# Expert stage of a ViT layer: 31 blocks of 256 rows and nine units of 128 rows in place of 39 blocks, four blocks beside the last pair's chain

## The reference, cut to what matters

```python
h = tok(x, W, gamma)                                  # 16 x 256 tokens, E = 256
h = h + attn(layernorm(h), Wq, Wk, Wv, Wg, Wa, ba, Wo, gn_w, gn_b)
xf = layernorm(h).reshape(4096, 256)
probs = softmax(xf @ w_router)                        # 8 experts
topk_w, topk_idx = top_k(probs, 2)
weights = sum(topk_w[..., None] * one_hot(topk_idx, 8), axis=1)
hid = gelu(einsum('te,ieh->tih', xf, w1) + b1)        # 256 -> 1024
y   = einsum('tih,ihe->tie', hid, w2) + b2            # 1024 -> 256
h = h + sum(y * weights[..., None], axis=1)
```

## Time and profile before

| | |
|---|---|
| median of three runs | 1410.64 us (1409.53 to 1412.68) |
| the profiled execution, its own time | 1410.71 us |
| its span in the profile | 1408.9 us |
| mean granted clock of TensorE | 0.975 of full speed |
| TensorE matmuls | 1296.7 us busy, 92% of the span, 9012 instructions |
| DVE | 923.7 us, 66% |
| ACT | 935.0 us, 66% |
| POOL | 458.5 us, 33% |
| HBM | 166.01 MB read, 29.96 MB written |
| weights of the experts | 78 loads of 1024 KB, median 7.3 us from issue to landing |

### The profile page before, as it was taken

How to read it: one execution, slowest core, us unless ns; L and a number is a source line. 1 busy time by engine, 2 the same in 40 slices (tenths; PEclk the granted TensorE clock), 3 DMA queues, 4 the chain that set the end, 5 groups by cost and what they waited for, 6 DMA issues and landing times. The chain is left out here.

```text
span 1408.9 us, 28979 instructions
## 1 busy us (share of the span) xinstructions
PE 1296.7 (92%) x9012; PEld 1108.5 (79%) x9012; DVE 923.7 (66%) x2290; ACT 935.0 (66%) x2197; POOL 458.5 (33%) x538
## 2 busy tenths in 40 slices
PE   4899999999999999999999995289999999999996
PEld 2666777877777777777777775289999999999996
DVE  3355556566566665665655666458888888888884
ACT  2557566557657556656656763168888888888884
POOL 3021211242142241231331423214444444444444
PEclk9999999999999999999999997589999999999998
DMA  5322322233233232232232323277777777777771
GB/s 179 106 94 68 101 92 91 72 115 100 74 104 100 80 117 80 97 111 75 95 98 81 94 91 105 83 232 215 216 231 215 232 232 235 228 223 234 214 232 35
DMA packets 126021, 192.86 MB, mean 137 GB/s; under 512 B 17216, under 2 KB 92192, under 8 KB 125792
## 3 DMA queue, kind: packets, MB, share of 16 engines
q1 hardware_dynamic: 111344, 174.52, 38.4%
q0 software_dynamic: 14592, 17.26, 5.6%
HBM read 166.01 MB, written 29.96 MB: 139 GB/s over the span
## 5 line engine op out<-in xcount | busy, mean ns | idle before, releaser
L844 PE MATMUL bank<-xn_sp,big_r 128*128 128x512 f32 x1152 | 313.4, 409 | 0.0
L844 PEld LDWEIGHTS bank<-xn_sp,big_r 128*128 128x128 f32 x1152 | 205.3, 189 | 54.1 <-issue 2.1
L1069 PE MATMUL bank<-big_r 128*128 128x256 f32 x1872 | 239.2, 284 | 0.9 <-DVE big_r L1501 0.9
L1069 PEld LDWEIGHTS bank<-big_r 128*128 128x128 f32 x1872 | 232.1, 193 | 1.3 <-DVE big_r L1501 1.3
L1193 DVE TENSOR_TENSOR att<-bank,dec_x 128x384 f32<-128x384 f32 x256 | 130.7, 552 | 119.8 <-PE bank L881 118.5
L594 ACT ACTIVATE dec_x<-dec_x,ncum 128x256 f32<-128x256 f32 (+1 forms) x512 | 189.7, 444 | 5.8 <-POOL dec_x L449 5.8
L449 POOL TENSOR_SCALAR_AFFINE_SELECT dec_x<-dec_x 128x256 f32<-128x256 f32 x256 | 102.1, 428 | 222.3 <-DMA dec_x<-cum_scratch 222.2
L1451 DVE TENSOR_TENSOR big_r<-big_f,big_r 128x512 fp32r<-128x512 f32 x236 | 162.7, 691 | 12.8
L502 POOL TENSOR_SCALAR mid_f<-mid_f,dec_x 128x256 f32<-128x256 f32 x78 | 90.8, 1169 | 228.0 <-DVE mid_f L1527 228.0
L738 ACT ACTIVATE mid_f<-bank,dec_x 128x256 f32<-128x256 f32 x312 | 145.0, 477 | 27.4 <-DVE big_r L1519 23.0
L1519 DVE TENSOR_TENSOR big_r<-mid_f,big_r 128x256 fp32r<-128x256 f32 x312 | 131.7, 423 | 39.6 <-ACT big_r L744 39.5
(11 more groups left out here) (154 smaller groups left out, 1968.7 us busy)
## 6 DMA issues: line engine op xcount, KB each, us to landing
big_f<-in_L_ffn_w SPq DMA_DIRECT2D x78, 1024.0 KB, 7.3
dec_x<-cum_scratch SPq DMA_DIRECT2D x128, 384.0 KB, 3.6
mid_f<-expert_rows SPq DMA_DIRECT2D x39, 261.0 KB, 7.4
tq<-in_L_ffn_b SPq DMA_DIRECT2D x39, 128.0 KB, 2.9
xt<-in_x SPq DMA_DIRECT2D x16, 256.0 KB, 3.7
h_scratch<-h SPq DMA_DIRECT2D x16, 256.0 KB, 2.4
h<-h_scratch SPq DMA_DIRECT2D x8, 512.0 KB, 4.5
out<-h SPq DMA_DIRECT2D x16, 256.0 KB, 3.9
```

The lines of the kernel that those rows point to most:

```text
L844: mm = pe.matmul(bank[target][:, :], wp[:, k, c * P:(c + 1) * P], xp[:, k, :], start=(k == 0 and j == 0), stop=(k == EC - 1 and j == 2))
L1069: mm = pe.matmul(bank[2 + c % HB][:, 0:BLK], wp[:, k, c * P:(c + 1) * P], xp[:, k, :], start=(k == 0 and j == 0), stop=(k == EC - 1 and j ...
```

## The change

**Counts.** The 8192 rows are cut in another way. There are `N1` + `N2` = 31 blocks of 256 rows, and `NU` = 9 units of at most 128 rows, which take the ends of the lists. `N1` = 10 blocks are laid out by a first table, from the lists of the first `EARLY` = 5 pairs of images; the other 21 blocks and the units by a second table from the full lists. 31 x 2 + 9 = 71 pieces of 128 rows is the most that 8192 rows in eight lists can need when only a list's last piece may be partly filled. Everything below is fixed when the program is built; the data decide only which expert and rows a block has.

**Three kinds of work.**

- *Early blocks* 0 to 3 are done in plain fp32: 16 products of 128 x 256 in each layer as `nc.tensor.matmul` of fp32 operands (`early1`, `early2`), with weights loaded straight to where they are used (`wf`, eight stretches in the room of attention weights that the last pair has done with; big_w is the same memory as big_r). There is no split by ACT and DVE. They are written in between the last pair's scores and its chain, on every engine.
- *Whole blocks* 4 to 21 are as before, in a loop of two (`whole_row`).
- *Rounds*: nine times a block and a unit. TensorE's `mixed_row` is the block's row, with the unit's rows turned and the first half of the unit's `layer1` in it; its `one_row` is the unit's rest, with the next block's rows turned and the first half of its `layer1` in it. A unit is plain fp32 too (`one1`: 16 products of 128 x 128, `one2`: eight of 128 x 256). ACT has only gelus in a unit's row, and four pieces of the split of the next block's `w2`, then the next block's rows.

**SP.** It sends the early blocks' loads from the last pair's fifth chunk on. The pads of all eight lists stand behind the loads of block 9. For the rounds a third staging place for `w1` (`w1_x`) lets the next block's `w1` go ahead; the unit's loads wait for the unit or block before.

**POOL.** The last pair's two `row_rsqrt` stand ahead of the scatters of pair 6, and its own scatters behind the adds of block 0. The scatter semaphores are split by pair (five and three).

**DVE.** `first_tables` (15 steps that wait for each other) stand in the last pair's first chunk; `last_tables` (40 steps) behind block 1's `keep_y`. `choose` and `first_half` of the last pairs move behind its group norm.

The diff, cut to its core:

```diff
-NT = (T * TOPK + X * (BLK - 1)) // BLK
+NF = 4
+N1 = 10
+NU = 9
+N2 = (T * TOPK // P + X - 1 - NU) // 2 - N1
+NB = N1 + N2 - NF
+NL = NB - NU
+NT = N1 + N2 + NU
...
+            def load_one(k):
+                e, r = expert(k.j), place(k.j)
+                sp.wait_ge(M["w1_lo"], WQ * NL)
+                sp.wait_ge(M["hid_ps"], HC * (k.j - 1))
+                load_w1(e, w1_f[1], "w1_in1")
+                sp.wait_ge(M["w2_lo"], WQ * NL)
+                sp.wait_ge(M["y_ps"], k.j - 1)
+                load_w2(e, w2_f[1], "w2_in1")
+                sp.wait_ge(M["wsel_done"], k.j - 1)
+                load_unit(r, 1)
+                load_b1(e, 1)
+                sp.wait_ge(M["y_done"], YB * (k.j - 1))
+                load_b2(e, 1)
...
+            for j in range(NF, N1):
+                load_whole(whole(j))
             sp.wait_ge(M["tb"], 2)
-            pad_list(0)
...
+            for e in range(X):
+                pad_list(e)
+            sp.wait_ge(M["pad_out"], 16 * (X + 1))
+            sp.wait_ge(M["scat2"], SCAT * (NPR - EARLY))
+            sp.wait_ge(M["scat3"], SCAT * (NPR - EARLY))
+            sp.wait_ge(M["tb"], 40)
...
+            def two_rounds(r):
+                m0, u0, m1, u1 = four(r)
+                load_one(u0)
+                load_rest(m1)
+                weights1_ahead(four(r + 1)[0], 0)
+                load_one(u1)
+                load_rest(four(r + 1)[0])
+                weights1_ahead(four(r + 1)[2], 1)
...
+            group_rsqrt(2 * NPR - 1)
+            row_rsqrt(2 * NPR - 2)
+            row_rsqrt(2 * NPR - 1)
+            scatter(NPR - 2, 0)
+            scatter(NPR - 2, 1)
+            pool.wait_ge(M["h2_out"], 32 * EARLY)
+            add_rows(whole(0), BS)
+            scatter(NPR - 1, 0)
+            scatter(NPR - 1, 1)
+            for j in range(1, NF):
+                add_rows(whole(j), BS)
...
+            def early1(j, c):
...
+                w = wf[j][0].rearrange("p (k n) -> p k n", k=EC)
+                for i in range(EC):
+                    mm = pe.matmul(bank[hbank[c % HB]][:, 0:BLK], w[:, i, c * P:(c + 1) * P], xe_u[j % 2][:, i, :],
+                                   start=(i == 0), stop=(i == EC - 1))
+                mm.then_inc(M["hid_ps"], 1)
...
+            def mixed_row(k, b_par, nxt):
+                layer1(k, b_par, two)
+                turn_rows(nxt, rows_f[1], 1)
+                layer2(k, b_par, one)
+                one1(nxt, one)
+                layer2(k, b_par, two)
+
+            def one_row(k, b_par, nxt):
+                one1(k, two)
+                turn_rows(nxt, rows_f[0], BS)
+                one2(k, one)
+                layer1(nxt, b_par, one)
+                one2(k, two)
```

More of the change, by code:

```diff
@@ L13 @@
+from collections import namedtuple
 from contextlib import ExitStack
@@ new lines, in vit_layer @@
+        b1_sb = [room(HC * i, HC) for i in range(2)]
+        te = room(16, NT)
+        cut1 = room(56, X * N1)
+        tmp1 = room(136, X * X).rearrange("p (a n) -> p a n", a=X)
+        nb1 = room(200, X)
+        cb1 = room(208, X)
+        w_1 = room(216, X)
+        f_1 = room(224, X)
+        tr1 = room(232, N1)
+        b2_sb = [room(256, E), tq[:, E:2 * E]]
+        NC1 = X * N1 + X * X + N1 * X
+        first = spare[:, BS * EW:BS * EW + NC1]
+        iob1 = first[:, 0:X * N1].rearrange("p (n a) -> p n a", a=N1)
@@ L208, in vit_layer @@
+        padf = table(1640, X)
         padi = sb("padi", [P, X], I32)
@@ L749, in blockrow, with whole_row @@
+            act.wait_ge(M["wo_ps"], 4 * NPR)
+            x_hi(first, 0)
+            for q in range(WQ):
+                w_hi("w2", w2_sp[0], w2_f[0], "w2_in0", 1, "y_ps", 2, q)
+            def whole_row(k, b_par, nxt):
+                activated(k, 0)
                 for c in range(HC):
                     if c + 1 < HC:
[L751 to L754 removed]
@@ new lines, in whole_row, with mixed_row @@
+                    if c == 3:
+                        x_hi(nxt, 1 - b_par)
+            def mixed_row(k, b_par, one, after):
+                activated(k, 0)
+                for c in range(HC):
+                    if c + 1 < HC:
+                        activated(k, c + 1)
+                    hidden_hi(k, c)
+                    if c == 3:
+                        x_one(one)
+                    if c >= HC - WQ and after is not None:
+                        w_hi("w1", w1_sp[1 - b_par], w1_stage[1 - b_par], ("w1_inx", "w1_in0")[b_par], after.w1n, "hid_ps", HC * k.j, c - (HC - WQ))
@@ L1107, in _ @@
+            one1(u0, two)
+            one2(u0, one)
+            one2(u0, two)
         @block.vector
@@ new lines, in _ @@
+            spread(p, 1)
+            affine(2 * p + 1)
+            choose(2 * p - 2)
+            affine_steps(p, 1)
+            choose(2 * p - 1)
+            first_half(p, 0)
+            gated(p, 1, 0)
+            first_half(p, 1)
+            gated(p, 1, 1)
+            y_lo(p, 1, 0)
+            keep_ranks(p - 1)
+            y_lo(p, 1, 1)
+            row_tails(whole(0), rows_u[0], BS)
+            weigh(p - 1)
+            place(p - 1)
+            residual(2 * p)
+            residual(2 * p + 1)
@@ new lines, in mixed_row, with one_row @@
+            def mixed_row(k, b_par, before, pieces, last):
+                for c in range(HC):
+                    hidden_lo(k, c)
+                    if c >= HC - WQ and not last:
+                        w_lo("w1", w1_sp[1 - b_par], w1_stage[1 - b_par], k.b + 1, c - (HC - WQ))
+                    if c == 2:
+                        keep_y(before, pieces)
+                    if c == 4:
+                        row_tails(k, rows_f[0], BS)
+            def one_row(k, b_par, before, after):
+                row_tails(k, rows_f[1], 1)
+                keep_y(before, BS)
+                if after is not None:
+                    for q in range(WQ):
+                        w_lo("w2", w2_sp[b_par], w2_f[0], after.b, q)
+                    x_lo(after, b_par)
```

998 lines of the change are left out of this document (697 added, 301 removed).

## The result

The changed kernel takes 1426.49 us (median of five runs, 1424.59 to 1435.46) against 1411.01 for the kernel before: 1.0121 times its time, 95% interval 1.0092 to 1.015. Five later runs gave 1427.09 and a ratio of 1.0115 (1.010 to 1.013). So it is slower by 1.2%, where 0.5% faster was forecast.

What follows compares the result with a forecast made beforehand. TensorE's products were taken to bound the expert stage. Start 939.4, blocks 217.6, pads 13.6, rounds 170.9, waits 46.1 and tail 14.0 gave a span of 1401.6, plus 1.8: forecast 1403 us, range 1355 to 1430.

Steps and rivals of the forecast that it cites:

- start of block 4's second half layer: End of the early part: 849.3 plus 76.3 us of TensorE work, 12.8 and 1.0 of waits, giving 939.4.
- blocks 4 to 21 with the pads: Loop of whole blocks: 18 x 12.09 = 217.6 us, plus 13.6 for eight pads delaying block 10's w1.
- rounds: waits for the unit's rows: Before each unit's turn, TensorE waits 3.1 us for rows queued behind w2, nine times: 27.9 us.
- rounds: slow products behind them: After each unit-row wait the lowered clock costs 0.8 us a round, about half of 1.7: 7.0 us.
- rounds: waits for the low part: In a unit's row, the next block's rows are split 1.4 us late by ACT and DVE, eight times: 11.2 us.
- rounds: the rest, TensorE's own work: Nine block rows 97.2 us, eight unit rows 68.4 and the last unit 5.3: 170.9 us.
- tail: After the last product, the last unit's scatter waits for the last block's: 14.0 us, against 12.2 before.
- The plain product: An fp32 product at 256 columns, two matmuls 0.215 us apart: 0.43 us against 0.36 for the split one.
- The wait for pair 6's scatters: Early part: DVE's norm of pair 7 waits for the buffer those scatters read, idling TensorE 8.8 us.
- The rival of dearer products: Early part and units: plain products cost some 0.27 us a half, giving 1434; chance 0.08.
- rounds that don't wait: Rounds: rows or small loads overtake w2, or TensorE is late enough; 42 of 46 us go, 1361; chance 0.25.
- The second rival: Rounds: both idle stretches halve the clock, losing 3.4 us a round, 23.6 more: 1427; granted clock near 0.85; chance 0.22.

Runs made afterwards that it cites:

- the later execution: The changed kernel run once more, unaltered; profiled execution 1427.06 us, median 1427.09 us.
- experiment 1: Changed kernel with the unit's rows sent just before its w2 instead of behind it, at the same moment: 1379.71 us, 0.9786 of the kernel before.
- experiment 4: Changed kernel with the eight pads sent two at a time in blocks 6 to 9 instead of all behind block 9: 1416.43 us.
- experiment 5: Changed kernel with POOL's order altered: four of pair 6's scatters before pair 7's first row norm, four between the two norms: 1419.23 us.
- experiment 8: On top of experiment 7, ACT and DVE split the next block's rows before its w2 in a unit's row: 1355.13 us, 0.9595 of before.
- experiment 3: Changed kernel with ten filler matmuls on TensorE ahead of each unit's turn: 1417.36 us, 1.0045 of the kernel before.
- experiment 2: Changed kernel with the unit's rows sent right behind its w1, before the wait for the last unit's end: 1379.87 us.
- experiment 6: Changed kernel with the nine rounds made plain rows of blocks, 39 blocks and no units: 1388.83 us.
- experiment 7: Changed kernel with the edits of experiment 2, experiment 4 and experiment 5 together: 1361.33 us.
- experiment 10: On top of experiment 8, the unit's rows sent ahead of both w1 of a round: 1359.84 us.

## Why the prediction was wrong

The steps of the sum, in the later execution:

| step | forecast, us | measured, us | difference |
|---|---|---|---|
| start of block 4's second half layer | 939.4 | 941.3 | +1.9 |
| blocks 4 to 21 with the pads | 231.2 | 231.1 | -0.1 |
| rounds: waits for the unit's rows | 27.9 | 41.5 | +13.6 |
| rounds: slow products behind them | 7.0 | 13.4 | +6.4 |
| rounds: waits for the low part | 11.2 | 11.0 | -0.2 |
| rounds: the rest, TensorE's own work | 170.9 | 174.7 | +3.8 |
| tail | 14.0 | 12.1 | -1.9 |
| span | 1401.6 | 1425.1 | +23.5 |

**Right.** The plain product at 0.43 us: groups of 16 matmuls, eight products, start 3.45 us apart (905.36 and 908.81 in the early part). The 128-column half: 16 of them (1212.85 to 1214.56) take 1.71 us, 0.107 each against 0.115 taken. The wait for pair 6's scatters, the pads in front of block 10's w1, the waits for ACT's split, the place and the releaser of the unit's waits: each was where the text put it, and experiments 1, 4, 5 and 8 each removed it by the edit that its mechanism names. The rival of dearer products falls; so does that of rounds that don't wait. Blocks 4 to 21 hit to 0.1 us by luck in part: 2.2 us less idle at the pads and 2.4 us of small waits that the forecast left out. In TensorE's own work in the rounds, 24 split products between plain ones took 2.95 us from start to start (1214.56 to 1217.51) and not 2.88.

**The step that failed** is the sentence "Rows of 0.13 MB behind w2 arrive at 0.3 + 5.0 + 0.5 = 5.8 and the turn starts at 6.0: 3.1 us, nine times". The mechanism is right (experiment 1 shows it), the size isn't: the turn starts 7.8 us after the row on the mean (6.6 to 9.3), and the wait is 4.6. The term that was too small is the 5.0 us for w2. It was the median of w1's landing in the old loop. The unit's own w2 took 5.5 to 8.5 us, 6.7 on the mean, in the first profile of the change, whose waits were 4.5 on the mean; the later profile doesn't tell the landing of these nine loads. The longest landing of before, 7.0, with a wait of 4.9, was the upper bound, and four of the nine waits lie above it (5.08 to 6.07).

Why w2 took longer stays open, but the trace narrows it. A load of 1 MB reports its landing in 16 parts. In the first profile the first part of the unit's w2 is there after 4.9 to 5.1 us in all nine rounds, and the last after 5.5 to 8.5: ten or more of the 16 are there within 5.7 us, and what makes the landing late is the last few. The DMA engines are full at that time. SP sends the next block's w2 3.7 us after the unit's (1203.49 after 1199.83), but this alone doesn't explain it: with the next one some 3.7 us behind, the unit's w2 landed in 5.5 us as well as in 7.4, and the last unit's, with none behind it, in 5.7.

**The second step** is the clock: "I take about half: 0.8 a round". Every one of the nine idles lowered it, at 1.5 us each (2.0 in the first profile). Half was a guess between one case for and one against, and it was low even for a wait of 3.1: of the five waits of 2.5 to 3.2 us in the profiles of experiments 3 and 4, four were followed by slow products, and the five lost 1.2 us on the mean, which makes 11 us for nine and not 7.

**Luck.** The second rival's 1427 is the measured time, and half of its mechanism is there: the first idle of a round lowers the clock each time, the second (1.3 us, at the split) never did. But of the 23.6 us that it adds, the clock gave 6.4; most of the rest came from longer waits. Its own sign says as much: it wanted a granted clock near 0.85 in the rounds, the forecast 0.96, and it was 0.91 (0.87 in the first profile).

**The chances.** The prediction put 0.63 on faster and 0.29 on slower, and slower came. Its range, up to 1430, held the time only because the rivals' times did; the forecast's own spread ended at 1416. The two terms stood near the middle of their bounds. With both at the upper end, nine waits of 4.9 and nine losses of 1.7, the working gives 16 + 8 us more: 1428. The spread left out that both go together, since a longer idle is also followed by slow products more surely. The lower end of the range leans on a short landing of w2 that no run shows: no unit's w2 landed in under 5.5 us in the change's first profile.

## What to carry to other kernels

Send what is wanted next before what is big: a load of 0.13 MB landed in 3.3 us ahead of 1 MB and was there 5.5 to 8.2 us after its issue behind it, at the same moment in the round, and exchanging the two in all nine rounds was worth 47 us. Price a load by its landing in the stage where it will run, not in the stage that the profile happens to show, and by its slow cases too, not only by its median. Count the slow products behind a wait as part of it: in the rounds here, waits of 2.5 us and more had them in all cases but one. A share of 0.60 over a stage doesn't say that the engines are free when it matters. A smaller unit of work has fewer products but as many weights to load, so look first at what its loads wait for, then at its arithmetic; and when a small edit undoes a loss, run it on the whole: the mended version took 1355 us, 4% less than the kernel before.

## What the hardware showed that was not expected

- The granted clock after an idle stretch of TensorE, over the nine rounds of the profiles of the change and experiments 1 to 8: after 0 to 1.3 us the next 24 products took 3.1 us every time; after 1.5 to 2.4 us they took 3.1 three times and 4.57 once; after 2.5 to 6.6 us 4.2 to 5.5, but for one case at 3.14 us with 3.12. The lower of the two levels, 1.2 of 2.4 GHz, holds for part of the group (granted 0.50 from 1208.20 to 1210.00 in the row shown, 1.00 in its twin). It isn't the length of one idle alone: the 3.14 us of experiment 4 left the clock up, and in the chain of experiment 10 an idle of 1.93 us, 6 us after one of 1.54, was followed by 7.3 us at a clock of 0.53.
- The unit's w2 took about as long where the rows went first: 6.8 us on the mean of nine (5.6 to 7.9) in experiment 1 against 6.7 (5.5 to 8.5) in the change's first profile. The small load gained 3.5 us, and the large one lost nothing that shows.
- The 16 parts of such a load don't land together: the first after 4.9 to 5.1 us in every round, the last up to 3.6 us later, which is when the load counts as landed.
- Executions of the kernels that keep the long waits in the rounds spread more: 1412 to 1428 (12 runs) in experiment 3, 1408 to 1422 (8) in 4 and 1414 to 1429 (12) in 5, against 2.6 us in experiment 1 and 3.5 without units (5 each). Fewer runs show less spread, so this is a hint.
